# Graph attention kernel: one-hots by edge stored in fp32, ScalarE weighs three slots of even groups

## The chip, the cores and the metric

The kernel runs on one core of one Trainium2 chip. The metric is the device time in microseconds of one execution of the whole program. Three runs of the kernel before gave 2498.72, 2498.89 and 2503.47 us; the median is 2498.89 us.

## The reference, cut to what matters

The reference takes 3125 nodes with 256 features and 50000 edges, sorted by destination. First it sums weighted rows over the edges, multiplies by a matrix and normalises. Then come two layers of graph attention (GATv2, 8 heads of 32) with a residual, and a last normalisation. One layer is

```
xl = (x @ Wl).reshape(n, H, C)
xr = (x @ Wr).reshape(n, H, C)
e = leaky_relu(xl[src] + xr[dst], 0.2)
score = einsum('ehc,hc->eh', e, att)
smax = segment_max(score, dst)
ex = exp(score - smax[dst])
denom = segment_sum(ex, dst)
out = segment_sum(ex / denom[dst] * xl[src], dst) + b
```

and every node also has an edge to itself.

## The kernel before, in words

Edges lie in slots of 128, one edge per partition; four slots make a group, 110 groups in all, and four groups make a chunk (28 of them, the last one with two groups). The slots are arranged so that each half of a group has edges of one tile of 128 destination nodes only.

The build stage (L540 to L737) runs over the 110 groups. For each it forms two one-hot matrices: by node (L629, DVE) and by edge (L707 and L723, ACT: the distance of each column from the edge's node, then 1 minus that, cut at zero). Both are written to DRAM as bf16, [128, 512] per group, by `keep` on SP (L542 to L547). GpSimd scatters weighted rows to DRAM meanwhile (L733), four scatters of 128 rows per group, from a ring of four groups of rows that DVE (L612, L632) and ACT (L700) fill. A stage that sums these rows and one that forms the linear parts follow; the change leaves them alone.

Each of the two layers has a message stage (L1006 to L1390). All engines run their own program over steps t, and semaphores alone tie them together:

- GpSimd gathers the rows of the sources, group by group, into a ring of 12 groups (L1132).
- PE `expand(t + 1)` adds the gathered rows and the rows of the destinations, taken by the one-hots by node (L1145, L1147, L1151). After it, in the same queue, stand the sums of group a = t - 6 (L1178): one-hot by edge times weighted rows, two accumulations of two slots each. In the first step after a chunk it also turns the ends of the scans over (L1163), and at a chunk's end it transposes the scores (L1190).
- DVE forms `product` (L1207 to L1214) and `score` (L1220) of group t, adds the sums of group a - 1 to the accumulator (L1264), weighs slots 2 and 3 of group a (`weigh`, L1079, called at L1306), and once per chunk does the scans for the running maximum (`ends` L1226, `carry` L1235 to L1238, `maximum` L1246) and the shift of the scores (`shift`, L1255 and L1256).
- ACT copies the linear part (`relu`, L1333, one group ahead), casts the one-hots by edge from bf16 to fp32 (`own`, L1339), weighs slots 0 and 1 of group a with one instruction per slot and head (`weigh_own`, L1347, 16 instructions) and once per chunk copies the carried ends (L1352) and takes the exponents (L1358, L1359).
- SP loads the one-hots, by node into `LBC` (L1112), by edge into `EDGE_HOTS` (L1093), four groups deep each.

The order on ACT in a step is relu, own, weigh_own, then the chunk's work. The first group of a chunk can only be weighed after that chunk's exponents, which need DVE's shift. PE takes the sums of group a when both weighings (`by_act`, `by_dve`) and the cast (`hots`) are there. Past the last group, two groups are summed in a step (`sums_at`).

`EDGE_HOTS` are the four bf16 slots in tile `HOTS`; the cast writes the two fp32 slots of tile `OH`, so it waits for the sums of two groups before (L1338).

Of the kernel before, what the change touches and what calls it, by code (L numbers as in the profile page):

```python
# [17 lines left out]
FP32 = mybir.dt.float32  # L18
# [6 lines left out]
P = 128  # L25
# [47 lines left out]
def build(nc, x, src, dst, edge_weight, W0, b0, gat, out):  # L73
# [56 lines left out]
    with top:  # L130
# [7 lines left out]
        step_d = dram("step_tables", [1, NI + P], I32)  # L138
        loc_d = dram("local_rows", [NI, P], BF16)
        to_tile_d = dram("hots_by_node", [NG, P, G * P], BF16)  # L140
        of_tile_d = dram("hots_by_edge", [NG, P, G * P], BF16)
        sup_d = dram("rows_by_src", [EP, UW], FP32)
        tab_d = dram("gather_table", [NP + 1, XW], FP32)
        line_d = dram("chunk_lines", [NW, LINE], FP32)
# [33 lines left out]
        LBC = sb("LBC", [P, 4, G * P], BF16)  # L178
        HOTS = sb("HOTS", [P, 2, G * P], FP32)
        OHT = HOTS  # L180
        EDGE_HOTS = HOTS[:, :, :].rearrange("p s n -> p (s n)").bitcast(BF16).rearrange("p (s n) -> p s n", s=4)
        OH = sb("OH", [P, 2, G, P], FP32)
        work = sb("work", [P, 2 * G * D + 2 * G * (D + H)], FP32)
        T = work[:, 2 * G * D:].rearrange("p (s w) -> p s w", s=2)
# [318 lines left out]
        with ctx:  # L503
# [26 lines left out]
            scattered = [sem(f"scattered{k}") for k in range(4)]  # L530
            AT = 4 * G * UW + NT * D
            BY_NODE = gath[:, AT:AT + G * P].bitcast(BF16).rearrange("p (s n) -> p s n", s=2)
            BY_EDGE = gath[:, AT + G * P:AT + 2 * G * P].bitcast(BF16).rearrange("p (s n) -> p s n", s=2)
            APART = work[:, 2 * G * D:2 * G * D + G * P]
            node_hot, apart, edge_hot = sem("node_hot"), sem("apart"), sem("edge_hot")
            node_kept = [sem(f"node_kept{k}") for k in range(2)]
# [467 lines left out]
        for layer, (_, _, _, bias) in enumerate(gat):  # L1004

            ctx, sem, ps = stage()  # L1006
            with ctx:
# [27 lines left out]
                def by_head(a):  # L1035
# [10 lines left out]
                    sem("by_row"), sem("ends_ready"), sem("in_rows"), sem("carried"), sem("copied"), sem("grow_ready"))  # L1046
                handed, maxima, final, shifted, exps, grown, risen = (
                    sem("handed"), sem("maxima"), sem("final"), sem("shifted"), sem("exps"), sem("grown"), sem("risen"))
                hots, by_act, by_dve, summed, added, chain, set_up = (
                    sem("hots"), sem("by_act"), sem("by_dve"), sem("summed"), sem("added"), sem("chain"), sem("set_up"))  # L1050
                def sums_at(t):

                    late = NG - LAG
# [15 lines left out]
                def at_chunk(u, n):  # L1069
                    i = K * u % (RING * G)  # L1070
                    return ROWS[:, i:i + n, :]

                def slots(q, g0, g1):
                    i = G * (q % RING)
                    return ROWS[:, i + g0:i + g1, :]
# [5 lines left out]
                with nc.Block() as block:  # L1081

                    @block.sync
                    def _(sp):
                        def lines(u):
                            if u >= 2:
                                sp.wait_ge(handed, u - 1)
                            sp.dma_start(LN[0:1, u % 2, :], line_d[u:u + 1, :]).then_inc(line_in[u % 2], 16)

                        def of_edges(a):  # L1090
                            if a >= 4:
                                sp.wait_ge(hots, a - 3)
                            sp.dma_start(EDGE_HOTS[:, a % 4, :], of_tile_d[a]).then_inc(edge_in[a % 4], 16)  # L1093

                        def ahead(sp):

                            sp.dma_start(VEC[:, 0, :], bias.rearrange("(a n) -> a n", a=1).broadcast_to([P, D])).then_inc(next_in, 16)
                            if layer < len(gat) - 1:
                                Wl, Wr, att = gat[layer + 1][0:3]
                                WBv = WB[:, :].rearrange("p (k n) -> p k n", k=2)  # L1100
                                sp.dma_start(WBv[:, :, 0:D], Wl.rearrange("(k p) n -> p k n", p=P)).then_inc(next_in, 16)
                                sp.dma_start(WBv[:, :, D:2 * D], Wr.rearrange("(k p) n -> p k n", p=P)).then_inc(next_in, 16)
                                sp.dma_start(VEC[:, 1, :], att.rearrange("h c -> (h c)").rearrange("(a n) -> a n", a=1).broadcast_to([P, D])).then_inc(next_in, 16)

                        for q in range(NG):
                            if q == NG // 2:
                                ahead(sp)
                            if q % WG == 0 and q:
                                lines(q // WG - 1)
                            if q >= 4:  # L1110
                                sp.wait_ge(expanded, q - 3)
                            sp.dma_start(LBC[:, q % 4, :], to_tile_d[q]).then_inc(node_in[q % 4], 16)  # L1112
                            if q >= LAG:
                                of_edges(q - LAG)
                        for a in range(NG - LAG, NG):
                            if a == NG - LAG + 2:
                                lines(NW - 1)
                            of_edges(a)
                        sp.wait_ge(expanded, NG)
                        sp.dma_start(XL, tab_d[0:NP, 0:D].rearrange("(t p) d -> p t d", p=P)).then_inc(rows_back, 16)  # L1120
                        sp.wait_ge(next_in, 64 if layer < len(gat) - 1 else 16)
                        sp.wait_ge(rows_back, 16)
# [16 lines left out]
                    def _(pe):  # L1139
# [17 lines left out]
                        for t in range(STEPS):  # L1157
                            if t + 1 < NG:
                                expand(t + 1)
                            u = chunk_at(t, 1)  # L1160
                            if u is not None:
                                pe.wait_ge(ends_ready, u + 1)
                                pe.transpose(by_head(LASTS)[:, :, 1:K + 1], FWD[:, P:P + 1], ident[:, :])  # L1163
                                pe.transpose(by_head(FIRSTS)[:, :, 1:K + 1], BWD[:, 0:1], ident[:, :]).then_inc(in_rows, 1)
                            v = chunk_at(t, 2)
                            if v is not None:
                                pe.wait_ge(maxima, v + 1)
                                pe.transpose(FINAL, BWD[:, 0:P], ident[:, :]).then_inc(final, 1)
                            for a in sums_at(t):
                                pe.wait_ge(hots, a + 1)  # L1170
                                pe.wait_ge(exps, 2 * (a // WG) + 2)
                                pe.wait_ge(by_act, a + 1)
                                pe.wait_ge(by_dve, a + 1)
                                for k in range(2):
                                    if a:
                                        pe.wait_ge(added, 2 * a - 1 + k)
                                    for g in (2 * k, 2 * k + 1):
                                        ins = pe.matmul(sums[k][:, 0:RW], OH[:, a % 2, g, :], slots(a, g, g + 1)[:, 0, :], start=(g % 2 == 0), stop=(g % 2 == 1))  # L1178
                                    ins.then_inc(summed, 1)
                            if u is not None:  # L1180
                                pe.wait_ge(copied, u + 1)
                                pe.transpose(CARRIED[:, 0:1], ENDS[:, 0:P], ident[0:1, 0:1])
                                pe.transpose(CARRIED[:, 1:2], ENDS[:, P:2 * P], ident[0:1, 0:1])
                                pe.matmul(FACTOR, LN[0:1, u % 2, KX:KX + P], DROP, start=True, stop=True).then_inc(grow_ready, 1)
                            u = chunk_at(t, 0)
                            if u is not None:
                                pe.wait_ge(scored, WG * u + groups(u))
                                if u:
                                    pe.wait_ge(shifted, 2 * u)
                                pe.transpose(BY_ROW, SC[:, u % 2].rearrange("p h k -> p (h k)"), ident[:, :]).then_inc(by_row, 1)  # L1190

                    @block.vector
                    def _(dve):
# [91 lines left out]
                        for t in range(STEPS):  # L1285
# [15 lines left out]
                            for a in batch:  # L1301
# [1 line left out]
                                    add_sum(a - 1, 0, tiles)  # L1303
                                last = a // WG == NW - 1
                                dve.wait_ge(exps, 2 * (a // WG) + (2 if last else 1))
                                weigh(dve, a, 2, G, slots(a, 2, G)[:, :, D:XW] if last else EXPS[:, G * (a % WG) + 2:G * (a % WG) + G, :]).then_inc(by_dve, 1)  # L1306
                                if u is not None and a == batch[0]:
                                    carry(u)
                                if a:
# [16 lines left out]
                    def _(act):  # L1326
# [5 lines left out]
                                act.wait_ge(scored, q - 1)  # L1332
                            act.activation(Tv[:, q % 2, :, :, C], slots(q, 0, G)[:, :, D:XW], ACT.Copy).then_inc(lin_ready, 1)  # L1333

                        def own(a):
                            act.wait_ge(edge_in[a % 4], 16 * (a // 4 + 1))
                            if a >= 2:
                                act.wait_ge(summed, 2 * (a - 1))  # L1338
                            act.activation(OH[:, a % 2].rearrange("p g n -> p (g n)"), EDGE_HOTS[:, a % 4, :], ACT.Copy).then_inc(hots, 1)  # L1339

                        def weigh_own(a):

                            act.wait_ge(exps, 2 * (a // WG) + 2)
                            for g in range(2):
                                R = slots(a, g, g + 1)[:, 0, :]
                                for h in range(H):
                                    ins = act.activation(R[:, h * C:(h + 1) * C], R[:, h * C:(h + 1) * C], ACT.Copy, scale=R[:, D + h:D + h + 1])  # L1347
# [25 lines left out]
                        for t in range(STEPS):  # L1373
# [1 line left out]
                            if t + 1 < NG:  # L1375
                                relu(t + 1)
                            for a in batch[:1]:
                                own(a)
                                weigh_own(a)
                            u = chunk_at(t, 1)  # L1380
                            if u is not None:
                                ends(u)
                            for a in batch[1:]:
                                own(a)
                                weigh_own(a)
                            u = chunk_at(t, 2)
                            if u is not None:
# [330 lines left out]
```

## Time and profile before

| what | value |
|---|---|
| median of three runs | 2498.89 us |
| the profiled execution | 2494.84 us |
| its span, first to last instruction | 2493.0 us |
| mean granted TensorE clock | 0.908 |
| busy: PE, DVE, ACT, GpSimd | 1900.3, 1739.0, 1364.3, 1516.8 us |
| build stage | about 100 to 670 us |
| message stage of the first layer | about 1043 to 1679 us |
| message stage of the second layer | about 1790 to 2425 us |

Busy time is the time in which an engine has an instruction under way. Its share of the whole span is a mean over stages with different limits, so each stage is read by itself. A clock of 1.00 means that TensorE had its full 2.4 GHz. Times of instructions are start and duration in microseconds from the start of the span.

### The profile page before, as it was taken

The page shows a single profiled execution, that of the slowest core. Times are in us where ns is not written, and L with a number is a line of the kernel's source. Part 1 is how long each engine was busy: PE and PEld are TensorE (multiplying, and loading weights), DVE is VectorE, ACT ScalarE, POOL GpSimd, SP SyncE. Part 2 cuts the span into 40 slices and gives each one's busy share as a digit, 9 for nine tenths or more (in the row PEclk, how much of TensorE's full clock was granted, in tenths as well). Part 3 has the DMA queues.
Part 4 walks back from the last instruction along what each step waited for, and adds up shares of the span by engine and source line. Part 5 has one row for each costly group of instructions (what it writes and reads, how often), then busy time and mean ns, then how long its engine had stood idle before and what let it go on. Part 6 is the DMA issues. An engine that isn't in the chain of part 4 may idle for free. (4 is left out here: it accounts for less than half of the span.)

```text
span 2493.0 us, 38225 instructions
## 1 busy us (share of the span) xinstructions
PE 1900.3 (76%) x8650; PEld 1362.9 (55%) x8650; DVE 1739.0 (70%) x3972; ACT 1364.3 (55%) x5328; POOL 1516.8 (61%) x1740
## 2 busy tenths in 40 slices
PE   0655556656389999689999999967479999999966
PEld 0443344444267776356666666644256666666644
DVE  9534333333256667479999999967289999999966
ACT  0255555555300003257887788873158888888873
POOL 3377777777700006877776777709877777777602
PEclk9777788887799999889999999988799999999988
DMA  3386575665488871255555555530155555555632
GB/s 98 82 193 167 170 165 172 167 169 167 106 258 262 266 245 63 80 157 154 159 149 164 152 150 153 142 81 33 57 158 158 155 155 151 152 152 150 142 93 89
DMA packets 272023, 369.92 MB, mean 148 GB/s; under 512 B 40436, under 2 KB 230902, under 8 KB 271831
## 3 DMA queue, kind: packets, MB, share of 16 engines
q1 hardware_dynamic: 207159, 195.75, 28.6%
q0 software_dynamic: 64512, 171.82, 24.6%
q8 instruction: 71, 1.16, 0.2%
q14 instruction: 121, 0.99, 0.1%
q10 hardware_dynamic: 160, 0.20, 0.0%
HBM read 272.59 MB, written 101.50 MB: 150 GB/s over the span
## 5 line engine op out<-in xcount | busy, mean ns | idle before, releaser
L1132 POOL DMA_INDIRECT gath<-gather_table,SRCI x880 | 835.5, 949 | 320.3 <-issue 266.0
L1347 ACT ACTIVATE gath<-gath 128x32 f32<-128x32 f32 x3520 | 766.5, 306 | 0.0
L1178 PE MATMUL p_sums<-gath,OH 128*128 128x272 f32 x1760 | 477.3, 412 | 107.4 <-DVE gath L1079 56.8
L733 POOL DMA_INDIRECT rows_by_src<-gath,node x440 | 440.3, 1001 | 136.7 <-issue 115.8
L667 PE MATMUL p_expd<-X,HOTS 128*128 x880 | 295.0, 496 | 231.6 <-DVE HOTS L626 228.4
L1178 PEld LDWEIGHTS p_sums<-gath,OH 128*128 128x128 f32 x1760 | 319.9, 194 | 222.6 <-issue 150.2
L667 PEld LDWEIGHTS p_expd<-X,HOTS 128*128 128x128 f32 x880 | 209.1, 249 | 306.1 <-issue 270.3
L1151 PE MATMUL p_expd<-node,LBC 128*128 x2640 | 329.4, 275 | 0.0
L1151 PEld LDWEIGHTS p_expd<-node,LBC 128*128 128x128 bf16 x2640 | 261.1, 99 | 59.8 <-issue 1.4
L1145 PE MATMUL p_expd<-gath,ident 128*128 128x512 f32 x440 | 236.3, 619 | 65.1 <-DMA gath<-gather_table,SRCI 64.9
L1220 DVE TENSOR_REDUCE scores<-work 128x32 f32<-128x1056 f32 x220 | 274.6, 1248 | 5.7
L811 PE MATMUL p_sums<-gath,OH 128*128 128x256 f32 x976 | 226.0, 387 | 45.9 <-DVE OH L784 45.5
L632 DVE CAST gath<-SRCI 128x4 f32<-128x4 int32 x110 | 22.9, 208 | 316.4 <-DMA rows_by_src<-gath,node 316.4
L700 ACT ACTIVATE gath<-p_expd,node 128x256 f32<-128x256 f32 x220 | 92.2, 470 | 267.1 <-DVE gath L632 179.0
L811 PEld LDWEIGHTS p_sums<-gath,OH 128*128 128x128 f32 x976 | 181.1, 191 | 90.8 <-DVE OH L784 37.4
L1264 DVE TENSOR_TENSOR node<-node,p_sums 128x272 f32 x440 | 187.9, 427 | 16.9 <-PE p_sums L1178 13.4
L875 POOL TENSOR_TENSOR gath<-gath 128x256 f32<-128x256 f32 x25 | 19.4, 777 | 266.8 <-ACT gath L897 266.6
L889 ACT ACTIVATE gath<-p_s 128x256 f32<-128x256 f32 x25 | 9.6, 383 | 283.1 <-PE p_s L921 283.1
L1209 DVE SCALAR_TENSOR_TENSOR work<-p_expd,VEC 128x512 f32<-128x512 f32 x220 | 149.4, 679 | 0.0
L1079 DVE TENSOR_TENSOR gath<-gath,p_factors 128x512 f32<-128x512 f32 x216 | 146.9, 680 | 0.0
L1147 PEld LDWEIGHTS p_expd<-gath,ident 128*128 128x128 f32 x440 | 84.9, 193 | 108.1 <-issue 108.1
L707 ACT ACTIVATE work<-iota_row,NLOC 128x128 f32<-128x128 f32 x440 | 139.5, 395 | 0.0
(290 smaller groups left out, 2732.6 us busy)
## 6 DMA issues: line engine op xcount, KB each, us to landing
gath<-rows_by_src SPq DMA_DIRECT2D x122, 514.0 KB
LBC<-hots_by_node SPq DMA_DIRECT2D x220, 128.0 KB
HOTS<-hots_by_edge SPq DMA_DIRECT2D x220, 128.0 KB, 2.4
LBC<-local_rows SPq DMA_DIRECT2D x110, 128.0 KB, 3.8
hots_by_node<-gath SPq DMA_DIRECT2D x110, 128.0 KB, 4.4
hots_by_edge<-gath SPq DMA_DIRECT2D x110, 128.0 KB, 2.7
gath<-gather_table,SRCI POOLq DMA_INDIRECT x880
rows_by_src<-gath,node POOLq DMA_INDIRECT x440, 4.1
```

The lines of the kernel that those rows point to most:

```text
L667: ins = pe.matmul(expd[q % 2][:, g // 2, (g % 2) * D:(g % 2 + 1) * D], OHT[:, q % 2, g * P:(g + 1) * P], Xv[:, bass.ds(tiles[g // 2], 1), ...
L733: pool.indirect_dma_start(sup_d[:, :], bass.IndirectOffsetOnAxis(POSI[:, i:i + 1], 0), U[:, q % 4, g, :], None, bounds_check=EP - 1, oob_i ...
L811: ins = pe.matmul(sums[s][:, 0:D], OH[:, s % 2, g, :], U[:, s, g, 0:D], start=(g == 0), stop=(g == G - 1))
L1079: return eng.tensor_tensor(R, R, by.unsqueeze(3).broadcast_to([P, g1 - g0, H, C]), ALU.mult)
L1132: pool.indirect_dma_start(ROWS[:, i % (RING * G), 0:XW], None, tab_d[:, :], bass.IndirectOffsetOnAxis(SRCI[:, i:i + 1], 0)).then_inc(gathe ...
L1145: pe.matmul(expd[q % 2][:, 0, :].rearrange("p (g n) -> p g n", g=2), ident[:, :], slots(q, 0, 2)[:, :, 0:D], start=True, stop=False)
L1151: ins = pe.matmul(expd[q % 2][:, g // 2, (g % 2) * D:(g % 2 + 1) * D], LBC[:, q % 4, g * P:(g + 1) * P], PARTS3[:, bass.ds(tiles[g // 2], ...
L1178: ins = pe.matmul(sums[k][:, 0:RW], OH[:, a % 2, g, :], slots(a, g, g + 1)[:, 0, :], start=(g % 2 == 0), stop=(g % 2 == 1))
L1209: dve.scalar_tensor_tensor(Tv[:, q % 2, 0:2, :, 0:C], expd[q % 2][:, 0, :].rearrange("p (g h c) -> p g h c", g=2, h=H), 0.0, SLOPES.unsque ...
L1220: dve.tensor_reduce(SC[:, q // WG % 2, :, k:k + G].rearrange("p h k -> p k h"), Tv[:, q % 2], AX, ALU.add).then_inc(scored, 1)
L1264: dve.tensor_tensor(ACC[:, bass.ds(j, 1), :], ACC[:, bass.ds(j, 1), :], sums[k][:, 0:RW].unsqueeze(1), ALU.add).then_inc(added, 1)
L1347: ins = act.activation(R[:, h * C:(h + 1) * C], R[:, h * C:(h + 1) * C], ACT.Copy, scale=R[:, D + h:D + h + 1])
```

## The change

One-hots by edge are kept in DRAM as fp32, so twice the bytes are stored in the build stage and loaded in each layer. They are loaded straight to where TensorE reads them: the two slots of `OH` and the two of `HOTS` make four. The cast on ACT goes, and with it the semaphore `hots`; SP now frees a slot by waiting for the sums (`summed`), and PE waits for the load itself. ACT weighs three slots of even groups and two of odd ones, DVE the rest.

```diff
-        of_tile_d = dram("hots_by_edge", [NG, P, G * P], BF16)
+        of_tile_d = dram("hots_by_edge", [NG, P, G * P], FP32)
-            BY_EDGE = gath[:, AT + G * P:AT + 2 * G * P].bitcast(BF16).rearrange("p (s n) -> p s n", s=2)
+            BY_EDGE = gath[:, AT + G * P:AT + 3 * G * P].rearrange("p (s n) -> p s n", s=2)
+                def hots_of(a):
+                    return OH[:, a % 4].rearrange("p g n -> p (g n)") if a % 4 < 2 else HOTS[:, a % 4 - 2, :]
+                def by_act_of(a):
+                    return 3 if a % 2 == 0 else 2
...
                         def of_edges(a):
                             if a >= 4:
-                                sp.wait_ge(hots, a - 3)
-                            sp.dma_start(EDGE_HOTS[:, a % 4, :], of_tile_d[a]).then_inc(edge_in[a % 4], 16)
+                                sp.wait_ge(summed, 2 * (a - 3))
+                            sp.dma_start(hots_of(a), of_tile_d[a]).then_inc(edge_in[a % 4], 16)
...
                             for a in sums_at(t):
-                                pe.wait_ge(hots, a + 1)
+                                pe.wait_ge(edge_in[a % 4], 16 * (a // 4 + 1))
...
-                                        ins = pe.matmul(sums[k][:, 0:RW], OH[:, a % 2, g, :], slots(a, g, g + 1)[:, 0, :], ...)
+                                        ins = pe.matmul(sums[k][:, 0:RW], hots_of(a)[:, g * P:(g + 1) * P], slots(a, g, g + 1)[:, 0, :], ...)
...
-                                weigh(dve, a, 2, G, slots(a, 2, G)[:, :, D:XW] if last else EXPS[:, G * (a % WG) + 2:G * (a % WG) + G, :]).then_inc(by_dve, 1)
+                                n = by_act_of(a)
+                                weigh(dve, a, n, G, slots(a, n, G)[:, :, D:XW] if last else EXPS[:, G * (a % WG) + n:G * (a % WG) + G, :]).then_inc(by_dve, 1)
...
-                        def own(a):
-                            act.wait_ge(edge_in[a % 4], 16 * (a // 4 + 1))
-                            if a >= 2:
-                                act.wait_ge(summed, 2 * (a - 1))
-                            act.activation(OH[:, a % 2].rearrange("p g n -> p (g n)"), EDGE_HOTS[:, a % 4, :], ACT.Copy).then_inc(hots, 1)
                         def weigh_own(a):
-                            for g in range(2):
+                            for g in range(by_act_of(a)):
...
-                                own(a)
                                 weigh_own(a)
```

## Rows read from the trace of the kernel before

**Rows 1.** Windows: window, its length, busy us per engine, granted clock, DMA share, GB/s.

```profile
500.00:600.00 100.00, 59.05 (x191) 44.24 (x190) 35.05 (x107) 52.58 (x139) 79.41 (x96) 0.79 0.58 167
...
1200.00:1600.00 400.00, 367.50 (x1935) 262.81 (x1935) 379.73 (x838) 322.54 (x1432) 283.91 (x300) 1.00 0.55 153
```

**Rows 2.** Waits, 1150 to 1550 us: engine, line, releaser: total us, times, longest.

```profile
ACT line L1352 <- DVE p_turned L1238: 50.6, 18, 3.0
...
PE p_sums L1178 <- ACT gath L1347: 13.4, 19, 0.8
...
DVE work L1207 <- PE p_expd L1151: 6.4, 19, 0.5
DVE forward L1226 <- PE p_turned L1190: 4.7, 18, 0.3
```

**Rows 3.** Timeline of a chunk: start, us, engine, line, op, tiles [idle before].

```profile
1302.86 0.28 DVE L1256 TENSOR_TENSOR gath<-p_turned,END 128x128 f32<-128x128 f32 x1
...
1303.71 0.61 ACT L1339 ACTIVATE OH<-HOTS 128x512 f32<-128x512 bf16 x1
...
1304.23 3.48 ACT L1347 ACTIVATE gath<-gath 128x32 f32<-128x32 f32 x16
...
1307.62 0.24 ACT L1333 ACTIVATE work<-gath 128x32 f32<-128x32 f32 x1
...
1308.07 2.07 PE L1178 MATMUL p_sums<-gath,OH 128*128 128x272 f32 x8 [0.83 <-ACT gath L1347]
...
1311.27 1.47 PE L1151 MATMUL p_expd<-node,LBC 128*128 x12
...
1312.78 0.42 DVE L1207 TENSOR_TENSOR work<-p_expd,gath 128x256 f32<-128x256 f32 x1 [0.46 <-PE p_expd L1151]
...
1314.73 0.42 DVE L1226 TENSOR_TENSOR_SCAN forward<-RST,p_turned 128x128 f32<-128x128 f32 x1 [0.26 <-PE p_turned L1190]
...
1318.74 0.42 ACT L1352 ACTIVATE line<-line 1x256 f32<-1x256 f32 x1 [2.96 <-DVE p_turned L1238]
```

**Rows 4.** Timeline, same chunk: DVE instructions whose starts give the spacing.

```profile
1313.12 0.68 DVE L1209 SCALAR_TENSOR_TENSOR work<-p_expd,VEC 128x512 f32<-128x512 f32 x1
...
1317.01 0.68 DVE L1079 TENSOR_TENSOR gath<-gath,p_factors 128x512 f32<-128x512 f32 x1
...
1317.61 0.42 DVE L1235 TENSOR_TENSOR_SCAN line<-lines,p_turned 1x136 f32<-1x136 f32 x1
```

**Rows 5.** All shifts of both layers (ns min/median/max, first to last), and the next shift.

```profile
L1256 DVE TENSOR_TENSOR gath<-p_turned,END x56: 211/279/284, 1087.7 to 2410.6; 128x128 f32<-128x128 f32 x54, 128x64 f32<-128x64 f32 x2
...
1324.51 0.28 DVE L1256 TENSOR_TENSOR gath<-p_turned,END 128x128 f32<-128x128 f32 x1
```

**Rows 6.** Timeline at the end of the first layer's message stage.

```profile
1645.47 0.33 PE L1168 MATMUL p_turned<-ident,backward 128*128 128x128 f32 x1 [2.37 <-DVE backward L1247]
...
1652.72 0.42 ACT L1352 ACTIVATE line<-line 1x256 f32<-1x256 f32 x1 [1.10 <-DVE p_turned L1238]
...
1657.24 3.96 PE L1178 MATMUL p_sums<-gath,OH 128*128 128x272 f32 x8 [1.25 <-ACT gath L1347]
...
1667.60 0.63 ACT L1339 ACTIVATE OH<-HOTS 128x512 f32<-128x512 bf16 x1 [1.79 <-PE p_sums L1178]
...
1675.74 2.07 PE L1178 MATMUL p_sums<-gath,OH 128*128 128x272 f32 x8 [1.84 <-ACT gath L1347]
```

**Rows 7.** Build stage: a wait total from 100 to 600 us, and the timeline.

```profile
POOL rows_by_src L733 <- DVE gath L612: 19.3, 4, 18.4
...
404.83 0.17 DVE L632 CAST gath<-SRCI 128x4 f32<-128x4 int32 x1 [2.93 <-DMA rows_by_src<-gath,node]
...
404.91 0.87 DVE L612 TENSOR_SCALAR gath<-p_expd,node 128x256 f32<-128x256 f32 x2
...
413.85 0.98 POOL L733 DMA_INDIRECT rows_by_src<-gath,node  x1 [0.19 <-issue]
```

**Rows 8.** Landing of the loads by edge (L1093), us min/median/max, 1150 to 1550.

```profile
DMA to landing us min/median/max: 1.9/2.6/3.5
```

More of the change, by code:

```diff
@@ L180, in build @@
         OHT = HOTS
-        EDGE_HOTS = HOTS[:, :, :].rearrange("p s n -> p (s n)").bitcast(BF16).rearrange("p (s n) -> p s n", s=4)
         OH = sb("OH", [P, 2, G, P], FP32)
@@ L1048, in build @@
                     sem("handed"), sem("maxima"), sem("final"), sem("shifted"), sem("exps"), sem("grown"), sem("risen"))
-                hots, by_act, by_dve, summed, added, chain, set_up = (
-                    sem("hots"), sem("by_act"), sem("by_dve"), sem("summed"), sem("added"), sem("chain"), sem("set_up"))
+                by_act, by_dve, summed, added, chain, set_up = (
+                    sem("by_act"), sem("by_dve"), sem("summed"), sem("added"), sem("chain"), sem("set_up"))
                 def sums_at(t):
@@ L1177, in _ @@
                                     for g in (2 * k, 2 * k + 1):
-                                        ins = pe.matmul(sums[k][:, 0:RW], OH[:, a % 2, g, :], slots(a, g, g + 1)[:, 0, :], start=(g % 2 == 0), stop=(g % 2 == 1))
+                                        ins = pe.matmul(sums[k][:, 0:RW], hots_of(a)[:, g * P:(g + 1) * P], slots(a, g, g + 1)[:, 0, :], start=(g % 2 == 0), stop=(g % 2 == 1))
                                     ins.then_inc(summed, 1)
@@ L1383, in _ @@
                             for a in batch[1:]:
-                                own(a)
                                 weigh_own(a)
```

## The prediction

> **What bounds the kernel now.** The row of each stretch comes first: between 1200 and 1600 us, inside the first attention layer, VectorE (DVE) is busy 380 of 400 us and TensorE (PE) 367, ScalarE (ACT) 323 and GpSimd 284, at a granted TensorE clock of 1.00, so at 2.4 GHz [rows 1]. DVE looks like the bound, and work taken from it looks like time won. The waits correct this [rows 2]. In 1150 to 1550 us, which hold about 18.7 chunks of four groups, DVE waits for PE twice in every chunk: 19 times ahead of the product (6.4 us) and 18 times ahead of the scans (4.7 us). PE in turn waits 19 times, once per chunk, for ScalarE's weighing (13.4 us). ACT has its long wait elsewhere: 50.6 us over 18 chunks, 2.8 us each, for the carry.
>
> The timeline of one chunk says where that happens [rows 3]. It is a closed loop, and I follow it by start times. The shift (L1256) starts at 1302.86 and ends at 1303.14; ACT takes the exponents, the relu, the cast of the one-hots (1303.71) and then 16 weighings of the first group of the new chunk (1304.23). PE waited 0.83 us for these and starts that group's sums at 1308.07. Its queue is in order, so the expansion of a later group stands behind these sums; its last twelve matmuls run from 1311.27 to 1312.74. DVE waited for exactly that and starts the product at 1312.78. Behind the expansion PE does the next group's sums and then the transpose of the scores, and DVE waits 0.26 us for it at 1314.73. From there DVE runs on without a wait that counts up to the next shift, at 1324.51 [rows 5]. So the period of a chunk is: shift, exponents, ACT's weighing of one group, PE, then DVE's rest. DVE's 95% is true, but the stretch between shift and product has no slack on the side of ACT and PE, and about 0.3 to 0.5 us on DVE's.
>
> The chunk repeats: 27 full shifts per layer (54 in two layers) [rows 5], 26 intervals per layer, 21.5 us each by the one shown (21.65 us).
>
> **The change part by part.** The groups are numbered a; a chunk of four begins with an even a, so its first and third group now get three slots on ACT and one on DVE, the second and fourth stay at two and two.
>
> *ACT, first group of a chunk.* The cast goes. From the start of the cast to the start of the first weighing are 1304.23 - 1303.71 = 0.52 us; its busy time, some 0.6, overlaps the next instruction. Eight weighings come. Sixteen take from 1304.23 to the next relu at 1307.62, 3.39 us, so 0.212 each [rows 3], and eight take 1.70. ACT is late by 1.70 - 0.52 = 1.18 us with this group. PE stood waiting for it already, so its sums start 1.18 later, the expansion too, and DVE's product starts 1.18 later. By the sum with a cast of 0.61 it would be 1.09.
>
> *DVE, first group.* One slot of 256 elements in place of two. No such weighing is in the trace. The nearest rows: two slots take 1317.61 - 1317.01 = 0.60 us from start to start, a 256-wide operation, the product's first, 1313.12 - 1312.78 = 0.34 [rows 3, 4]. The saving is 0.26 (0.30 if it halves). For this group it lies between the shift and the product, where DVE waits anyway: it turns into wait and brings nothing.
>
> *DVE, third group.* The same 0.26 us, but behind the last wait of the loop, where DVE sets the pace. It counts. ACT's eight extra weighings there stand ahead of its wait for the carry. Counted from the shift, ACT is done with the first group after 5.8 us, with the second after 5.8 + 0.12 + 3.39 = 9.3, with the third after 9.3 + 0.12 + 5.09 = 14.5, and ACT gets the carry at 1318.74 - 1303.14 = 15.6 now and 16.5 then [rows 3] (its wait of 2.8 us in rows 2 is cut to about two). Hidden; if that cover were gone it would cost up to 1.70 per chunk.
>
> *Sum of a chunk:* +1.18 - 0.26 = +0.92 us. Over 26 chunks and two layers: 52 x 0.92 = 47.8 us.
>
> *End of a layer.* The last six groups come two in a step and hang on ACT. Six casts go (6 x 0.52 = 3.1), 24 weighings come (3 x 1.70 = 5.1), and the wait of the cast for the sums of two groups before goes, since no tile is overwritten: 1.79 us in the first layer. The first group's extra weighings fall into a wait for the carry of 1.10 [rows 6]. Net: 5.1 - 3.1 - 1.8 - 1.1 = -0.9; I take -1 per layer, so -2, with 0 and -5 as bounds.
>
> *Loads and their wait.* SP now waits for the sums of the group four before, where it waited for the cast. Behind it in SP's queue stands the load of the one-hots by node of the next group, which needs the expansion that PE does behind those very sums, so it is not held longer; likewise the chunk's line. The load is issued four groups (21 us) ahead of its use and lands in a median of 2.6 us for 128 KB, 3.5 at most [rows 8]. Twice the bytes take between 2.6 and, if everything doubles, 7 us. Hidden. In the first groups of a layer the gathers are short of time, and the first loads stand beside them: 0 to +5 us per layer, I take 0, since the DMA engines are busy 0.55 of the time [rows 1] with room for it.
>
> *The build stage (100 to 670 us).* ACT writes 512 elements as before, in fp32, and 256 KB are stored per group. GpSimd's scatters set the pace: it is busy 79 of 100 us, and the rest is the gap of 0.3 us ahead of each issue [rows 1]; it waited for DVE only four times, 18.4 of 19.3 us at once at the start [rows 7]. DVE does wait for scatters that land, but look at the cushion: the landing at 404.83 lets DVE scale the group whose scatter starts at 413.85; scaling ends 0.95 us later, 8.1 us early [rows 7]. Doubled stores would have to delay scatters by more than that. I take 0.
>
> **Total.** 47.8 - 2 = +46 us. On the profiled execution, 2494.84 us, that is 2541; the median of the runs, 2498.89, lies 4 us higher, and so do I: 2545 us, slower by 1.8%.
>
> **The rivals.**
>
> *DVE is the bound after all (faster).* Place: all 55 even groups of a layer. If ACT's extra work hid in its waits (the carry's alone are 50.6 us of 400 [rows 2]), each would bring 0.26 us, 110 x 0.26 = 29 us: 2470. It decides if PE could start the first group's sums 1.18 us later without DVE noticing. For it: DVE at 95%. Against it: PE's wait for ACT and DVE's wait for PE are there already, in each chunk, and nothing lies between. 6%.
>
> *Gain and loss cancel.* If only about a third of the 1.18 us arrived at DVE, as after gathers that set the pace, the time would be within 0.2% of 2499. It needs slack that rows 3 don't show. 3%.
>
> *The clock falls in the longer gap.* PE will wait 0.7 to 0.8 + 1.18 = 1.9 to 2.0 us ahead of the first group's sums, in each chunk. At the end of the layer a wait of 2.37 us stands before a stretch in which the eight matmuls of a pair of sums took 3.96 us in place of 2.07, the lower level, 1.2 GHz [rows 6]. If each chunk paid these 1.9 us once, 52 x 1.9 = 98 us: 2642. Against it: after a wait of 1.84 us in a stretch where PE is busy half the time the same eight took 2.07 [rows 6]. The Trainium skill (TensorE: Matmul & The Clock Gate, section HAM oscillation) tells of loops in which each wait between bursts brings the half clock back; by that rule this rival would hold, and the row with 1.84 us speaks against it. 8%, a few chunks of it go into the range.
>
> *Stores or loads set the pace.* If landings in the build stage grew by over 8 us, GpSimd would wait; each 0.4 us per group is 44 us over 110 groups: 2588. 3%.
>
> *The change doesn't do what it says.* The cast and its wait leave the code, nothing else could keep them; there is no room for this.
>
> **How the numbers follow.** My case has 80%. Its own bounds: per chunk 0.83 (cast at 0.61) to 1.18 (no saving on DVE), so 43 to 61 us, -5 to 0 at the ends, 0 to +10 for the first groups, on a base of 2495 to 2499: roughly 2533 to 2570. With a little room below for partial absorption, the range is 2526 to 2571; the rivals, 20% together, lie outside. 0.2% is about what a measurement of this kernel can tell from no change. Slower: 80 + 8 + 3 = 91%; within: 3%; faster: 6%.
>
> **What would show it.** Shifts 22.4 us apart in place of 21.5. DVE's wait ahead of the product at 1.6 to 1.9 us, PE's wait for ACT near 1.9, once per chunk; the wait for the transpose still 0.26. DVE's busy share down to 90%, 440 more weighings per layer on ACT and no cast. The build stage as long as before, GpSimd's waits the same. I am wrong if shifts come closer than 21.5, if DVE's wait doesn't grow (a slack that I didn't see), if the granted clock between 1200 and 1600 us leaves 1.00, or if scatters wait.

## The result and the profile after

The changed kernel takes 2589.91 us in the median of four runs (2586.21 to 2603.97), the kernel before 2498.80 (2497.45 to 2503.47). The ratio is 1.037, with a 95% interval of 1.034 to 1.041. It is slower, as forecast, but by 91 us and not by 46, and it lies outside the range of 2526 to 2571 us. The profiled execution took 2603.97 us, its span 2602.2; of the four it is the slowest, and all that is read from its trace below is 109 us above the profiled execution of before.

Line numbers of the message stage are higher by 7 on SP, PE and DVE now (L1263 is the shift that was L1256, L1214 the product, L1233 and L1242 the scans, L1086 VectorE's weighing, L1185 the sums) and by 2 on ScalarE (L1349 the weighing, L1341 the relu, L1354 the carry's copy).

The windows that answer [rows 1], with the build stage from 100 to 600 us: window, length, busy us of PE, weight load, DVE, ACT and GpSimd, granted clock, DMA share, GB/s.

```profile
100.00:600.00 500.00, 294.80 (x942) 217.60 (x942) 179.65 (x521) 269.01 (x707) 389.94 (x472) 0.78 0.70 195
1200.00:1600.00 400.00, 350.67 (x1751) 247.80 (x1752) 338.21 (x761) 317.49 (x1513) 260.43 (x272) 0.96 0.58 161
```

The build stage does its 390 us of GpSimd work in 500 us as before. In the layer, VectorE fell from 380 to 338 us of 400, TensorE from 367 to 351, and nobody took over as the busiest: the engines wait for each other longer. The granted clock is no longer 1.00 but 0.96.

The waits between 1150 and 1550 us, which answer [rows 2]: total us, times, longest.

```profile
POOL gath L1139 <- PE p_sums L1185: 63.4, 46, 3.3
...
ACT line L1354 <- DVE p_turned L1245: 50.1, 17, 3.9
DVE work L1214 <- PE p_expd L1158: 37.8, 18, 3.0
PE p_sums L1185 <- issue: 35.6, 34, 2.0
...
DVE forward L1233 <- PE p_turned L1197: 4.4, 17, 0.3
...
DVE line L1242 <- issue: 3.0, 17, 0.2
```

VectorE's wait ahead of the product went from 6.4 to 37.8 us, the wait for the transpose stayed 0.26 each time, and a new one of 0.17 us appeared ahead of the carry's scan (L1242). TensorE's wait ahead of the first group's sums is now shown under "issue" (34 times: 17 of about 1.9 us ahead of the first group and 17 of 0.17 us ahead of the third).

One chunk of the layer, which answers [rows 3 to 5]: start, duration.

```profile
1302.78 0.28 DVE L1263 TENSOR_TENSOR gath<-p_turned,END 128x128 f32<-128x128 f32 x1
...
1303.51 0.25 ACT L1341 ACTIVATE work<-gath 128x32 f32<-128x32 f32 x1
1303.64 5.20 ACT L1349 ACTIVATE gath<-gath 128x32 f32<-128x32 f32 x24
...
1308.74 0.25 ACT L1341 ACTIVATE work<-gath 128x32 f32<-128x32 f32 x1
...
1309.04 2.07 PE L1185 MATMUL p_sums<-gath,OH 128*128 128x272 f32 x8 [1.88 <-issue]
...
1310.95 1.02 PE L1152 MATMUL p_expd<-gath,ident 128*128 128x512 f32 x2
...
1313.75 0.42 DVE L1214 TENSOR_TENSOR work<-p_expd,gath 128x256 f32<-128x256 f32 x1 [1.77 <-PE p_expd L1158]
...
1315.70 0.42 DVE L1233 TENSOR_TENSOR_SCAN forward<-RST,p_turned 128x128 f32<-128x128 f32 x1 [0.26 <-PE p_turned L1197]
...
1317.98 0.41 DVE L1086 TENSOR_TENSOR gath<-gath,p_factors 128x256 f32<-128x256 f32 x1
...
1318.21 0.27 PE L1171 MATMUL p_turned<-ident,backward 128*1 128x128 f32 x1
...
1318.57 0.42 DVE L1242 TENSOR_TENSOR_SCAN line<-lines,p_turned 1x136 f32<-1x136 f32 x1 [0.17 <-issue]
...
1325.48 0.28 DVE L1263 TENSOR_TENSOR gath<-p_turned,END 128x128 f32<-128x128 f32 x1
```

The loop is the one that was foreseen: 24 weighings take 1308.74 - 1303.64 = 5.10 us, the sums start behind them, the expansion behind the sums, the product 10.97 us after the shift, and the next shift 11.73 us behind the product, as long as before (1324.51 - 1312.78). The shifts of this chunk are 22.70 us apart.

But the next chunk takes 24.50. Its part of TensorE's queue in the timeline:

```profile
1331.88 2.97 PE L1185 MATMUL p_sums<-gath,OH 128*128 128x272 f32 x8 [2.03 <-issue]
1334.65 1.86 PE L1152 MATMUL p_expd<-gath,ident 128*128 128x512 f32 x2
```

The windows of the two chunks, columns as above:

```profile
1302.78:1325.48 22.70, 19.80 (x105) 14.12 (x104) 20.00 (x46) 18.69 (x89) 16.32 (x17) 1.00 0.63 171
1325.48:1349.98 24.50, 21.48 (x105) 14.93 (x104) 20.05 (x46) 18.68 (x89) 15.44 (x16) 0.93 0.55 153
```

The same eight matmuls of the sums take 2.97 us in place of 2.07 and the two of the expansion 1.86 in place of 1.02. The granted clock of the chunk is 0.93. The gap does not tell the two kinds apart: but for the first chunk of each layer it is 1.87 to 2.03 us long ahead of the sums in both, and two of the quick chunks have 2.02 and 2.03. In the slow ones the eight matmuls of the sums take between 2.72 and 3.76 us, where all eight at the lower level, 1.2 GHz, took 3.96 [rows 6], so the stretch at the lower level lies differently over them each time. All shifts of both layers make this table (the intervals between full shifts, 26 per layer):

```
kernel    sum of the 52 intervals   near 22.70   near 24.4 (with 25.5 at a layer's start)
before    1118.8 us                 all 21.46 to 21.66, but one of 22.85
after     1226.6 us                 26           26
```

The difference is 107.8 us, of the 109.1 between the profiled executions. So what was paid is (22.69 - 21.48) x 52 = 63 us for the longer loop and 26 x 1.66 = 43 us for chunks at a lower clock. The stage before the first shift is 1.2 us longer, the stretch between the layers 2.8 longer, the end 2.5 shorter. The median run, 14 us below the profiled one, would have about 18 slow chunks by the same reckoning, and the quickest of the four about 15; that is worked out, not seen.

### The profile page after: what moved, and what is told of

It reads as the page before. It is cut to its first block and busy times, and to the rows that moved or that the text cites. A ratio compares the mean times of both kernels' runs of the same rounds, so it can differ in the third digit from the quotient of the medians.

```text
span 2602.2 us, 38669 instructions
## 1 busy us (share of the span) xinstructions
PE 1949.9 (75%) x8650; PEld 1388.1 (53%) x8650; DVE 1719.1 (66%) x3972; ACT 1437.5 (55%) x5988; POOL 1523.7 (59%) x1740
## 3 DMA queue, kind: packets, MB, share of 16 engines
q14 instruction: 124, 1.02, 0.1%
## 5 line engine op out<-in xcount | busy, mean ns | idle before, releaser
L1139 POOL DMA_INDIRECT gath<-gather_table,SRCI x880 | 844.1, 959 | 414.8 <-issue 247.4
L1349 ACT ACTIVATE gath<-gath 128x32 f32<-128x32 f32 x4400 | 953.1, 306 | 0.1
L1185 PE MATMUL p_sums<-gath,OH 128*128 128x272 f32 x896 | 268.3, 450 | 112.9 <-issue 96.8
L1152 PE MATMUL p_expd<-gath,ident 128*128 128x512 f32 x440 | 251.7, 656 | 64.1 <-DMA gath<-gather_table,SRCI 63.9
L1185 PE MATMUL p_sums<-gath,HOTS 128*128 128x272 f32 x864 | 243.4, 416 | 56.3 <-DVE gath L1086 31.2
L1185 PEld LDWEIGHTS p_sums<-gath,OH 128*128 128x128 f32 x896 | 182.3, 214 | 166.1 <-issue 129.5
L810 PEld LDWEIGHTS p_sums<-gath,OH 128*128 128x128 f32 x976 | 180.4, 191 | 91.9 <-issue 34.5
L1185 PEld LDWEIGHTS p_sums<-gath,HOTS 128*128 128x128 f32 x864 | 154.5, 193 | 127.3 <-issue 70.9
L1214 DVE TENSOR_TENSOR work<-p_expd,gath 128x256 f32<-128x256 f32 x220 | 92.1, 419 | 150.7 <-PE p_expd L1158 148.8
```

Of the source, the lines that this page charges most:

```text
L810: ins = pe.matmul(sums[s][:, 0:D], OH[:, s % 2, g, :], U[:, s, g, 0:D], start=(g == 0), stop=(g == G - 1))
L1139: pool.indirect_dma_start(ROWS[:, i % (RING * G), 0:XW], None, tab_d[:, :], bass.IndirectOffsetOnAxis(SRCI[:, i:i + 1], 0)).then_inc(gathe ...
L1152: pe.matmul(expd[q % 2][:, 0, :].rearrange("p (g n) -> p g n", g=2), ident[:, :], slots(q, 0, 2)[:, :, 0:D], start=True, stop=False)
L1185: ins = pe.matmul(sums[k][:, 0:RW], hots_of(a)[:, g * P:(g + 1) * P], slots(a, g, g + 1)[:, 0, :], start=(g % 2 == 0), stop=(g % 2 == 1))
L1214: dve.tensor_tensor(LAST, expd[q % 2][:, 1, D:2 * D].rearrange("p (h c) -> p h c", h=H), slots(q, G - 1, G)[:, 0, 0:D].rearrange("p (h c) ...
```

## The experiments

Five questions stood: whether the loss is ScalarE's work or the doubled bytes, where VectorE's 0.26 us went, whether the slow chunks come from the gap in TensorE's work, whether one group of the chunk carries all, and what a better version is. Times are read against the kernel before in the same series, 2502 us in the first and 2504 in the last. The first chunk of each layer is given apart, since it is up to some 3 us longer than the rest.

**Two slots on ScalarE everywhere.** fp32 one-hots and no cast, but no third slot.

```diff
-                    return 3 if a % 2 == 0 else 2
+                    return 2
```

> The change with two slots on ScalarE for every group: fp32 one-hots, no cast, no third slot. Theory A (the loss is ScalarE's extra weighing on the loop of each chunk): the loop is 0.52 us shorter than before, shifts 20.96 us apart instead of 21.48, no chunk longer than 22, granted clock 1.00 between 1200 and 1600 us; 52 x 0.52 = 27 us less than before, about 2472 us. Theory B (the doubled bytes of the stores and loads cost time): the time stays well above before, 2520 to 2590 us, with chunks over 22 us. If VectorE's own work is the bound once the wait is gone, 2480 to 2499.

Measured: 2479.55 us, ratio 0.992 (0.990 to 0.994), chunks of 21.32 to 21.56 us, 21.33 most often (21.02 and 22.78 for the first of each layer), granted clock 1.00 from 1200 to 1600 us. So the doubled bytes are not the loss: stores and loads of the changed kernel are in this one too, and it beats the kernel before. Theory B is gone. But the chunk is 21.33, not 20.96, so only 0.15 of the 0.52 us came through. Its waits from 1150 to 1550 us say why:

```profile
PE p_sums L1185 <- DVE gath L1086: 18.9, 37, 0.6
...
DVE forward L1233 <- PE p_turned L1197: 10.6, 19, 0.7
```

TensorE no longer waits for ScalarE, but still twice a chunk for VectorE's weighing, once just ahead of the shift (0.59 us); everything up to the transpose stands behind that in its queue. VectorE's wait ahead of the product is gone (6.4 us before), but its wait for the transpose grew from 4.7 us to 10.6: what went from one wait came nearly whole in the other.

**Three slots in the third group alone.**

```diff
-                    return 3 if a % 2 == 0 else 2
+                    return 3 if a % 4 == 2 else 2
```

> Three slots on ScalarE in the third group of a chunk alone, two in the other three. Theory A, with the reading that VectorE's 0.26 us saved there runs into the wait for TensorE's transposes ahead of the carry: the same time as with two slots everywhere, within 3 us, shifts 20.96 us apart. The step of the prediction (the saving counts): 0.26 us a chunk less than with two slots everywhere, 52 x 0.26 = 14 us less, shifts 20.7 us apart.

Measured: 2484.42 us, ratio 0.993 (0.991 to 0.995), chunks of 21.32 to 21.40 us (22.70 and 22.71 for the first of each layer). The 0.26 us saved on VectorE bring nothing, 14 us less didn't come; the intervals of this and the last kernel overlap, though the medians differ by 4.9 us, where 3 were allowed for. The chunks don't hold that difference: all 52 take 1112.2 us here and 1111.8 there. The spacing of 20.96 us missed here as it did there.

**The third group's saving by itself, on the kernel before.** Slot 2 of the third group is weighed by nobody: work is left out, nothing is added.

```diff
-                                weigh(dve, a, 2, G, ...)
+                                n = 3 if a % 4 == 2 else 2
+                                weigh(dve, a, n, G, ...)
```

> The same as e7_less_on_dve, on another chip. The kernel before, where VectorE weighs slot 3 alone in the third group of a chunk and nobody weighs slot 2, which is left out. The prediction's step: shifts 21.22 us apart. The carry waits for the transposes in TensorE's queue: 21.48, with a wait of 0.2 to 0.3 us ahead of the carry's scan. (The last interval of a layer was 21.52 on the other chip.)

Measured: 2500.57 us in one run beside 2503.56 of before (2499.31 to 2504.05), chunks of 21.46 to 21.64 us (23.19 and 23.29 for the first of each layer). The place, in this kernel's timeline:

```profile
1319.33 0.41 DVE L1079 TENSOR_TENSOR gath<-gath,p_factors 128x256 f32<-128x256 f32 x1
...
1319.55 0.27 PE L1164 MATMUL p_turned<-ident,backward 128*1 128x128 f32 x1
...
1319.92 0.42 DVE L1235 TENSOR_TENSOR_SCAN line<-lines,p_turned 1x136 f32<-1x136 f32 x1 [0.17 <-issue]
```

The weighing is shorter, and the carry's scan starts 0.59 us after the weighing's start as ever [rows 4], because it needs the two transposes (L1163, L1164) that TensorE does behind an expansion. The wait of 0.17 us isn't marked with TensorE as its releaser; that it is the transpose follows from the times and from the wait in `carry`. In the kernel before, the same transpose ends 0.10 us ahead of the scan (which starts at 1317.61) as well:

```profile
1317.24 0.27 PE L1164 MATMUL p_turned<-ident,backward 128*1 128x128 f32 x1
```

**Three slots in the first group alone.**

```diff
-                    return 3 if a % 2 == 0 else 2
+                    return 3 if a % 4 == 0 else 2
```

> The same as e5_first_only, since its call fell on a chip on which the kernel before took 2984 us in place of 2499. Three slots on ScalarE in the first group of a chunk alone. All of the loss on the first group: shifts 22.70 us apart, or 24.36 where the clock falls, about 2590 us. The third group has a share: 22.4 or 22.9 in place of 22.70.

Measured: one run of 2599.10 us; chunks of 22.66 to 22.88 (25) and of 24.4 us (27, with 25.45 at the second layer's start), 1226.7 us in all 52, where the changed kernel has 1226.6. The first group carries the whole loss, and the third group has no share. It is a single execution, but the length of its two kinds of chunk doesn't rest on its total.

**Matmuls in the gap.** The changed kernel with six matmuls on the identity ahead of TensorE's wait in each first group.

```diff
                             for a in sums_at(t):
+                                if a % WG == 0 and a and t < NG:
+                                    pe.wait_ge(added, 2 * a)
+                                    for r in range(6):
+                                        pe.matmul(sums[1][:, 384:512], ident[:, :], ident[:, :], start=True, stop=True)
```

> The changed kernel, with six matmuls of 128 columns on the identity, written to columns of the sums' bank that nobody reads, on TensorE ahead of its wait for ScalarE in the first group of each chunk. They need some 1.2 us of the 1.88 us in which it stood idle. Theory C (the chunks of 24.36 us are those in which that idle gap brought the clock down; those of 22.70 have only the longer loop): all chunks take 22.70, the granted clock is 1.00 between 1200 and 1600 us, and 26 x 1.66 = 43 us go: 2560 us beside 2590 or so. If the long chunks come from loads or from contention: as many chunks of 24.4 as before, or more, and no time saved.

Measured: 2559.51 us, ratio 1.024 (1.022 to 1.025) where the changed kernel has 1.037; all chunks 22.66 to 22.70 except the first of each layer (24.40 and 25.51). Two rows of its timeline:

```profile
1317.11 1.60 PE L1180 MATMUL p_sums<-ident 128*128 128x128 f32 x12
1319.14 2.07 PE L1189 MATMUL p_sums<-gath,OH 128*128 128x272 f32 x8 [0.42 <-issue]
```

Its window:

```profile
1200.00:1600.00 400.00, 375.44 (x2053) 274.86 (x2052) 351.53 (x791) 331.92 (x1582) 269.39 (x282) 1.00 0.61 167
```

Useless work, and 30 us less (48 between the profiled executions, since that of the changed kernel is the slowest of its four). The wait for ScalarE is as long, the sums start 6.26 us behind the shift in both, TensorE merely isn't idle in it, and the slow chunks are gone with the clock back at 1.00. They were the clock's, brought on by the gap.

**The third slot on the kernel before.** bf16 one-hots and the cast stay.

```diff
-                            for g in range(2):
+                            for g in range(3 if a % 2 == 0 else 2):
...
-                                weigh(dve, a, 2, G, ...)
+                                n = 3 if a % 2 == 0 else 2
+                                weigh(dve, a, n, G, ...)
```

> The kernel before (bf16 one-hots, cast on ScalarE) with the third slot alone: three slots on ScalarE in even groups. Theory A: the loop is 8 x 0.212 = 1.70 us longer, so chunks of 21.48 + 1.70 = 23.18 us at full clock. TensorE's gap ahead of the first group's sums grows to 2.4 us; by theory C more chunks than in the changed kernel lose the clock, up to all, for 23.18 + 1.66 = 24.84. Time: 2587 us with none slow, 2673 with all. Theory B (the bytes cost): with bf16 there is no loss, about 2500 us or less.

Measured: 2631.15 us, ratio 1.052 (1.050 to 1.054). Chunks of 23.16 (27 of them) and 24.8 us (25, with 25.88 and 26.15 at the layers' starts): 21.48 + 1.68 and 1.65 more. The dose fits on the loop's side, 1.70 foreseen and 1.68 seen. On the clock's side it is open. Between the profiled executions the share of slow chunks did not grow with a gap of 2.37 us in place of 1.88 (25 beside 26), but the changed kernel's was the slowest of its four. By an estimate from the times of the four runs each, at 1.66 us a slow chunk, the changed kernel had 15 to 26 slow chunks and this one 22 to 26. "Up to all" is wrong either way. From the third chunk of a layer on, no two slow chunks follow each other here, where the changed kernel has up to three in a row. What decides which chunk is slow stays open.

**A version that beats both.** Two slots everywhere, and TensorE waits for VectorE's slots only ahead of the half of the sums that uses them.

```diff
-                    return 3 if a % 2 == 0 else 2
+                    return 2
...
                                 pe.wait_ge(by_act, a + 1)
-                                pe.wait_ge(by_dve, a + 1)
                                 for k in range(2):
+                                    if k:
+                                        pe.wait_ge(by_dve, a + 1)
                                     if a:
                                         pe.wait_ge(added, 2 * a - 1 + k)
```

> The same as e6_split_waits, on another chip. Two slots on ScalarE everywhere, and TensorE waits for VectorE's weighing only ahead of the sums' second half. The wait held the loop: shifts 20.9 to 21.0 us apart, 2455 to 2465 us. VectorE's own work is the bound: 21.3, 2480 us.

Measured: 2462.30 us, ratio 0.983 (0.982 to 0.985). Chunks of 21.1 us in the first layer and 21.02 in the second (20.91 and 22.60 for the first of each). The wait held the loop, with a little less behind it than reckoned (20.9 to 21.0). From 1200 to 1600 us VectorE is now busy 386 us of 400:

```profile
1200.00:1600.00 400.00, 367.17 (x1973) 265.37 (x1971) 386.00 (x852) 291.26 (x1381) 292.47 (x308) 1.00 0.65 182
```

Three of these kernels (three slots in the first group alone, less on VectorE in the third group, this one) had been run in an earlier series, with these expectations:

> The changed kernel with three slots on ScalarE in the first group of a chunk alone; the third group is back at two. If all of the loss hangs on the first group's weighings: shifts 22.7 us apart, or 24.4 where the clock falls, both kinds present, as in the changed kernel; one run near 2590 us. If the third group has a share in it (its extra weighings, or VectorE's saving that counts): 22.4 or 22.9 us apart in place of 22.7.

> The kernel before with 0.26 us less on VectorE in the third group of each chunk and nothing else: VectorE weighs slot 3 alone there, and nobody weighs slot 2, which is left out. By the prediction's step (behind the last wait VectorE sets the pace) shifts are 21.22 us apart in place of 21.48. By the reading of the changed kernel's trace (the carry waits for two transposes that stand behind an expansion in TensorE's queue) they stay 21.48 apart, with a wait of 0.2 to 0.3 us ahead of the carry's scan.

> The changed kernel with two slots on ScalarE everywhere, and with TensorE's wait for VectorE's weighing moved from ahead of the sums' first half (slots 0 and 1, ScalarE's) to ahead of the second half (slots 2 and 3, VectorE's). With two slots everywhere TensorE waits for VectorE's weighing twice a chunk, 0.59 and 0.44 us, and the shifts are 21.33 us apart, not 20.96. If that wait is what holds the loop there: 20.9 to 21.0 us apart, some 20 us less than the 2480 of two slots everywhere, 2455 to 2465 us. If VectorE's own work is the bound: 21.3 as before, 2480 us.

In that series the kernel before took 2983.74 us (2974.46 to 2997.39), the three kernels 3045.54 and 2996.63 (one run each) and 2961.68, a ratio of 0.993 (0.991 to 0.995) for the split waits. Most of their chunks took between 24 and 34 us, with stretches of up to some 4 us in which an engine waited for nothing that the profile names. So these times are not set against the expectations. What slowed that series isn't known. Its chip bears the same number as that of the first series, in which the kernel before took 2502 us, so the "another chip" of the later expectations is true of the last series, but isn't shown to be the cause. Only the last interval of each layer was undisturbed, 22.7, 21.52 and 21.01 us, the values of the later runs.

## Why the prediction went wrong, step by step

**The bound.** Right. The loop from the shift over ScalarE's first weighing and TensorE's queue to the product was read before the change, and the two kernels with the third slot in one group alone settle it: in the first group it costs everything, in the third nothing. Shifts were foreseen 22.4 us apart; they are 22.70 (or 24.4), and the two steps that failed are the difference.

**ScalarE, first group: +1.18.** Right, 1.20 measured: 5.10 - 3.39 = 1.71 for the eight weighings, and from the start of the relu to the first weighing 0.13 us now where 0.64 stood, so 0.51 for the cast.

**VectorE, first group: turns into wait.** Right: its wait ahead of the product is 1.77 us where 0.27 to 0.46 stood.

**VectorE, third group: -0.26, "behind the last wait of the loop, where DVE sets the pace. It counts."** This step failed. What the saving is worth lies within 0.03 us of nothing, by each of three pairs: on the kernel before, with two slots in the other groups, and with three in the first. No wait was shown ahead of the carry's scan in the kernel before, and from that I took slack on TensorE's side. In fact the two finished almost together: the weighing's 0.60 us ended about when the transposes came (0.10 us ahead of the scan). A wait of zero length says that two things arrive together as well as it says that one is early. Cost: 52 x 0.26 = 14 us.

**The clock.** This step failed too, and it is the one that took the time out of the range: the filled gap gives 2559.51 us, well inside. The prediction's sum has nothing for it. The mechanism was named, with a price (1.9 us a chunk, 2642 us if in each) and a place, and given 8% as an alternative instead of a share in the sum. It came in half the chunks at 1.66 us: 43 us in the profiled execution, about 30 in the median one. The granted clock between 1200 and 1600 us left 1.00, which the prediction had set as a sign of being wrong. The mistake was to treat it as all or nothing. I had one row for and one against it [rows 6], a lower clock after 2.37 us of waiting and the full one after 1.84, and the gap forecast, 1.9 to 2.0, lay between them; with rows that disagree around the value wanted, the case "in some of the chunks" is the likely one and belongs in the sum. The Trainium skill (TensorE: Matmul & The Clock Gate, section HAM oscillation) tells of a loop in which waits of some 3 to 5 us between bursts bring the half clock back in every round, and of another in which frequent short idle stretches, given without a length, make the clock go to and fro. Here, with gaps of 1.87 to 2.03 us, the trace shows a lower clock in 26 chunks of 52 and none in the rest, so it agrees with the second and not with "every round". The prediction's "by that rule this rival would hold" left out how long the waits of the first loop are.

**Loads, stores, the new wait.** Right: no wait for a load by edge shows, a load of 256 KB lands in a median of 2.9 us (2.6 for 128 KB before) in the kernel with two slots everywhere, and the build stage is as long as it was at a DMA share of 0.70. The wait of 1.88 us under "issue" isn't one for the load either: with the same loads and two slots TensorE waits 0.18 us at that place.

**The ends of the layers.** -2 foreseen; +1.2, +2.8 and -2.5 us were seen in the stretches outside the chunks, +1.5 together, so about nothing. Its terms (casts, weighings, the two waits) were not measured one by one.

**The sum.** By the measured terms: 52 x 1.21 = 63, 26 x 1.66 = 43, ends +1.5: 108 us, for 109 in the profiled executions. The forecast of 46 lacks the 14 us of the third group, which it had taken off, 43 of the clock, and 3 to 4 at the ends.

**The faster rival** (VectorE is the bound, 2470) fell: its busy share in the layer dropped by ten points, and the time rose.

## What to carry to other kernels

Ask of each piece of work that is moved between engines in which step of the loop it lands: the same 1.70 us on ScalarE cost 1.68 us in the first group of a chunk (1.2 where the cast went) and nothing in the third, and the same 0.26 us off VectorE was worth nothing in either. Where an operation starts without a wait, find out when its inputs came, before counting on a saving ahead of it. A longer idle gap on TensorE can be paid twice, once as time and once as clock; and a wait should stand ahead of the first instruction that needs it, here the second half of a sum, which with the cast gone gave a ratio of 0.983.

## What the runs showed of the hardware

In the changed kernel, a gap of 1.87 to 2.03 us ahead of TensorE's sums, in a loop in which it is busy 19.8 of 22.7 us, brought a lower clock in half of the rounds of the profiled execution (26 of 52): in one of them 2.97 us in place of 2.07 for the sums and 1.86 in place of 1.02 for the expansion's first two, and 1.66 us more for the round. A gap of 2.37 us did so in 25 of 52. The gap alone doesn't decide: at the start of the first layer of the kernel before, the sums behind a gap of 2.47 us took 2.07 us, at full clock. With six useless matmuls in the changed kernel's gap, 1.6 us long, leaving 0.42 us idle, the clock never fell after a layer's first chunk.
